# Layer 1 of a two-layer attention kernel: the key mask moves from TensorE to VectorE, the conditioning's scale and shift from VectorE and GpSimd to ScalarE

## The reference, cut to what matters

```python
xn = _ln(x, ln_w, ln_b)
q = xn @ Wq + bq
k = xn @ Wk + bk + (1.0 - src_mask) * -1000000.0
q = softmax(q.reshape(b, t, h, dh), axis=-1)
k = softmax(k.reshape(b, t, h, dh), axis=1)
v = ((xn @ Wv + bv) * src_mask).reshape(b, t, h, dh)
att = einsum('bnhd,bnhl->bhdl', k, v)
y = einsum('bnhd,bhdl->bnhl', q, att).reshape(b, t, d)
scale, shift = split((silu(emb) @ W_emb + b_emb)[:, None, :], 2, axis=2)
hh = _ln(y, ln2_w, ln2_b) * (1.0 + scale) + shift
return x + silu(hh) @ W_out + b_out
```

## Time and profile before

| what | value |
|---|---|
| median of 3 runs | 1095.91 us (1095.82 to 1096.64) |
| the profiled execution, its own time | 1097.78 us |
| its span, first to last instruction | 1096.0 us |
| TensorE busy | 1054.8 us, 96% of the span |
| VectorE, ScalarE, GpSimd busy | 759.8, 591.6, 448.6 us |
| mean granted TensorE clock | 0.993 of full speed |

### The profile page before, as it was taken

How to read it: one execution, slowest core, us unless ns; L and a number is a source line. 1 busy time by engine, 2 the same in 40 slices (tenths; PEclk the granted TensorE clock), 3 DMA queues, 4 the chain that set the end, 5 groups by cost and what they waited for, 6 DMA issues and landing times. The chain is left out here.

```text
span 1096.0 us, 25953 instructions
## 1 busy us (share of the span) xinstructions
PE 1054.8 (96%) x8696; PEld 909.8 (83%) x8696; DVE 759.8 (69%) x1326; ACT 591.6 (54%) x1960; POOL 448.6 (41%) x783
## 2 busy tenths in 40 slices
PE   6999999999999999999999999999999999999995
PEld 4878888888888888888887778888888888888884
DVE  4656766676666766667678787777777777777764
ACT  5366667776677766776588443433343443434431
POOL 3242434334343343433343344444444444444432
PEclk9999999999999999999999999999999999999997
DMA  8824110111101111011102211111111111111011
GB/s 275 256 84 141 42 61 24 62 62 41 60 24 62 62 41 59 25 62 63 43 23 98 95 50 33 40 55 57 57 57 57 57 57 57 52 52 39 31 38 58
DMA packets 46017, 71.65 MB, mean 65 GB/s; under 512 B 10256, under 2 KB 14448, under 8 KB 45968
## 3 DMA queue, kind: packets, MB, share of 16 engines
q1 hardware_dynamic: 45968, 71.02, 20.3%
HBM read 54.19 MB, written 16.79 MB: 65 GB/s over the span
## 5 line engine op out<-in xcount | busy, mean ns | idle before, releaser
L1276 PE MATMUL bank<-xt_hi,w_hi 128*128 128x256 f32 x768 | 228.4, 297 | 3.1 <-DVE xt_lo L893 3.1
L1277 PE MATMUL bank<-xt_lo,w_hi 128*128 128x256 f32 x768 | 218.5, 284 | 0.0
L1278 PE MATMUL bank<-xt_hi,w_lo 128*128 128x256 f32 x768 | 218.3, 284 | 0.0
L454 POOL TENSOR_SCALAR stat<-stat 128x1 f32<-128x1 f32 x128 | 34.5, 270 | 441.8 <-DVE stat L884 417.7
L613 ACT ACTIVATE prob<-prob,neg_max 128x128 f32<-128x128 f32 x512 | 198.7, 396 | 6.7 <-DVE neg_max L907 6.6
L632 ACT ACTIVATE th<-z_s 128x512 f32<-128x512 f32 x64 | 40.5, 633 | 249.9 <-POOL z_s L488 249.8
L1276 PE MATMUL bank<-w_hi,xt_hi 128*128 128x512 f32 x384 | 158.3, 412 | 1.0 <-DVE w_lo L835 1.0
L1276 PEld LDWEIGHTS bank<-xt_hi,w_hi 128*128 128x128 f32 x768 | 148.9, 194 | 9.1 <-DVE w_lo L835 4.8
L1278 PE MATMUL bank<-w_hi,xt_lo 128*128 128x512 f32 x384 | 150.5, 392 | 0.0
L1277 PE MATMUL bank<-w_lo,xt_hi 128*128 128x512 f32 x384 | 149.8, 390 | 0.0
L1277 PEld LDWEIGHTS bank<-xt_lo,w_hi 128*128 128x128 f32 x768 | 148.6, 193 | 0.0
(11 more groups left out here) (130 smaller groups left out, 2203.3 us busy)
## 6 DMA issues: line engine op xcount, KB each, us to landing
x_in<-in_x_dram SPq DMA_DIRECT2D x32, 256.0 KB, 2.8
x_res<-in_x_dram SPq DMA_DIRECT2D x32, 256.0 KB, 2.9
between_layers<-x_res SPq DMA_DIRECT2D x32, 256.0 KB, 2.0
x_in<-between_layers SPq DMA_DIRECT2D x32, 256.0 KB, 2.8
x_res<-between_layers SPq DMA_DIRECT2D x32, 256.0 KB, 2.8
out_dram<-x_res SPq DMA_DIRECT2D x32, 256.0 KB, 2.6
room<-in_L_cond_W_emb_dram SPq DMA_DIRECT2D x8, 512.0 KB, 7.3
prob<-in_L_cond_emb_w_dram SPq DMA_DIRECT2D x4, 512.0 KB, 7.5
```

The source lines that it names most:

```text
L454: pool.tensor_scalar(v[:, 8:9], v[:, 7:8], EPS, None, ALU.add).then_inc(s[a_in].sem, 1)
L1276: pe.matmul(o, a_hi, b_hi, start=start, stop=False)
L1277: pe.matmul(o, a_hi, b_lo, start=False, stop=False)
L1278: return pe.matmul(o, a_lo, b_hi, start=False, stop=stop)
```

## The change

On TensorE the four mask matmuls of a pair go, and with them `mask_wide`, `ones_parts`, `mask_parts` and what fills them. The mask bias of layer 1 is now saved to DRAM as layer 0's is, and `load_mask_pair` (SP) fetches it for each pair, spread over all partitions, into the one tile `mask_pair` (128 x 256). In `k_soft` VectorE takes each key block out of the bank itself, adding the key bias and the mask in one instruction (`scalar_tensor_tensor`), before it takes the maximum; ScalarE's `k_out` stays in layer 0 alone. In layer 1 `film_scale` and `add_shift` go; ScalarE's new `film1` does scale and shift in four instructions of 128 columns out of the bank, ahead of the tanh. In the mixed step `k_soft(f, 0)` stands earlier in VectorE's list.

```diff
@@ SP
+            def load_mask_pair(f):
+                sp.wait_ge(*done(s["kb_out"], f + (-GROUP)))
+                at = f + (-B)
+                flat = mask_bias[1].rearrange("(o b) p -> o (b p)", o=1)
...
+                sp.dma_start(mask_pair[:], row.broadcast_to([P, N])).then_inc(s["mask_pair_in"].sem, 16)
...
                 if k:
                     load_back(1, k, 1)
+                if n:
+                    load_mask_pair(n)
+                if k:
                     store(1, k, 0)
@@ GpSimd
                 if k:
                     norm2(k, 1)
-                    add_shift(1, k, 0)
-                    add_shift(1, k, 1)
@@ ScalarE
+            def film1(k, b):
+
+                at = k + (b - B)
+                act.wait_ge(*done(s["h_pe"], k + b))
+                act.wait_ge(*done(s["s_full"], k + (b - 2)))
+                for c in range(C):
...
+                    last = act.activation(z_s[:, b, c * P:(c + 1) * P], bank[SECOND["H"][b]][:, c * P:(c + 1) * P],
+                                          ACT.Identity, bias=shift, scale=scale)
+                last.then_inc(s["z_full"].sem, 1)
...
                 if f:
-                    k_out(1, f, slot, 0)
                     k_exps(f, slot, 0)
...
                 if f:
-                    k_out(1, f, slot, 1)
                     k_exps(f, slot, 1)
...
                 if k:
+                    film1(k, 0)
                     tanh(k, 0)
                 if f:
                     q_exps(f, slot, 0)
                 if k:
                     s_high(k, 0)
+                    film1(k, 1)
                     tanh(k, 1)
@@ VectorE
             def k_soft(f, slot, pair):
-                dve.wait_ge(*done(s["ka_out" if pair == 0 else "kb_out"], f))
+                if pair == 0:
+                    dve.wait_ge(s["mask_pair_in"].sem, (f + (-B)).value() * (16 // GROUP) + 16)
+                out = s["ka_out" if pair == 0 else "kb_out"]
+                dve.wait_ge(*done(s["ka_pe" if pair == 0 else "kb_pe"], f))
...
+                for j in range(2):
+                    c = 2 * pair + j
+                    last = dve.scalar_tensor_tensor(out=kv[:, c, :], in0=from_bank[:, j, :], scalar=col[:, 1, KB, c:c + 1],
+                                                    in1=mask_pair[:], op0=ALU.add, op1=ALU.add)
+                last.then_inc(out.sem, GROUP)
+                dve.wait_ge(*done(out, f))
...
@@ VectorE, step_mixed
                 softmax(k, 0, (3,))
+                dve.wait_ge(bias_dve, TURN[1, WK])
+                k_soft(f, slot, 0)
                 stats1(n, 0)
                 softmax(k, 1, (0, 1, 2))
                 output(FIRST, late + (-1), 1)
                 softmax(k, 1, (3,))
-                k_soft(f, slot, 0)
                 k_soft(f, slot, 1)
@@ VectorE, step1
                     y_norm(1, k, 1 - slot, 1)
-                    film_scale(1, k, 0)
...
                     s_low_part(k, 0)
-                    film_scale(1, k, 1)
@@ TensorE, project
-                    if l == 1:
...
-                        pe.matmul(o, ones_parts[:], cols, start=True, stop=False)
```

More of the change, by code:

```diff
@@ L79, in build @@
     WQ, WK, WV, WO = range(4)
-    mask_bias = nc.dram_tensor("mask_bias", [B, P], F32, kind="Internal").ap()
+    mask_bias = [nc.dram_tensor(f"mask_bias{l}", [B, P], F32, kind="Internal").ap() for l in range(2)]
     middle = nc.dram_tensor("between_layers", [B, T, D], F32, kind="Internal").ap()
@@ L365, in start @@
                 load_wide(1, WO, OUT_BIAS[1])
[L366 to L370, removed]
+                sp.wait_ge(mask_cut, 4)
+                sp.dma_start(mask_bias[1], mask_tmp[1][:, P:2 * P]).then_inc(mask_saved, 16)
                 sp.wait_ge(bias_sum_pe, 3)
@@ L441, in _ @@
             pool.memset(ones_32nd[:], 1.0 / 32).then_inc(once, 1)
[L442 to L447, removed]
+            pool.wait_ge(once, 4)
             pool.tensor_tensor(pick[:], ident[:, 0:2 * B], ident[:, 2 * B:4 * B], ALU.add).then_inc(consts, 1)
@@ L626, in y_t_out @@
                 act.activation(y_t[:], bank[FIRST["PV"][b]][:], ACT.Copy).then_inc(s["pv_out"].sem, 1)
+            def film1(k, b):
[3 more added lines that the diff above has]
+                for c in range(C):
+                    scale, shift = (film_ab[:, 1, i, c, at.const:at.const + 1] if at.reg is None
+                                    else film_ab[:, 1, i, c, bass.ds(at.value(), 1)] for i in range(2))
+                    last = act.activation(z_s[:, b, c * P:(c + 1) * P], bank[SECOND["H"][b]][:, c * P:(c + 1) * P],
+                                          ACT.Identity, bias=shift, scale=scale)
+                last.then_inc(s["z_full"].sem, 1)
             def tanh(k, b):
@@ L712, in step0 @@
                 exps(k, 1, (3,))
[L713 removed]
+                k_out(f, slot, 1)
                 if i == G - 2:
@@ L720, in step0 @@
                 y_t_out(k, 1)
+                if i == 0:
+                    act.wait_ge(mask_saved, 32)
                 tanh(k, 0)
@@ L1047, in step0 @@
                 if late:
-                    film_scale(0, late + (-1), 1)
+                    film_scale(late + (-1), 1)
                 if i == G - 3:
```

84 lines of the change are left out of this document (35 added, 49 removed).

## The result

The changed kernel takes 1105.26 us (median of 6 runs, 1104.44 to 1106.32) against 1096.73 us before: a ratio of 1.0076, 95% interval 1.0063 to 1.0089. It is slower by 0.8%, and the forecast was 1092.0 us.

What follows compares the result with a forecast made beforehand. TensorE was taken to bound layer 1 (busy 434.68 of 440 us), the chain's latency the end. Terms 0 - 0.2 - 0.55 - 3.1 = -3.9 us from 1095.9 gave 1092.0 us; range 1086.5 to 1100.0.

Steps and rivals of the forecast that it cites:

- rival 5: The mask's fetch comes late and `k_soft` waits for it in each step, by 1 us: 1105 us; chance 0.03.
- Masks on TensorE: In each layer 1 step, dropping TensorE's mask matmuls saves 0.40 us (0.16 to 0.48).
- The wait for the low part: At sequence 1's output, `film1` brings VectorE's low part earlier and TensorE's wait goes: -0.31 us a step.
- The late chain: VectorE's evictions add 0.88 us before the second `turn_yn`, where 0.45 were free: TensorE waits 0.43 us a step.
- The meetings: At the second `turn_yn`, silu against GpSimd: whoever starts first, half the steps each; wait 0.43 or 1.0, taken as 0.72 us.
- rival 3: Difference and silu both hold up GpSimd; TensorE waits some 1.4 us at the second `turn_yn`: 1101.1 us; chance 0.15.
- A step: Steps 17 to 29: -0.40 - 0.31 + 0.72 = 0.0 us each, nothing over the 13.
- The mixed step: `k_soft` puts 1.76 us ahead of `y_norm(k, 0)`, which had 1.34 us idle: +0.6 us (0 to 1.2).
- From there to step 17: Step G: masks -0.24, waits at `turn_yn` and outputs -1.07, later `norm2(k, 1)` +0.5; -0.8 us in all.
- Step 30 and the end: Step 30 gains 0.55 us, as `norm2` is not late; in the last step outputs come earlier: -3.1 us.
- The mask's fetch and the start: Fetch of `mask_pair` at no cost, issued early; at the start TensorE waits for weights and inputs: nothing (0 to -0.5).

Runs made afterwards that it cites:

- film_only: The kernel before with `film1` (scale and shift on ScalarE), TensorE's masks and ScalarE's `k_out` as they were: 1089.56 us, ratio 0.9926.
- idle_reduce: The changed kernel plus one VectorE reduction, its result unread, ahead of the first sequence's query maximum: 1093.33 us, ratio 0.9962.
- sum_in_bank: The changed kernel with query plus bias left in the bank, so maximum and difference read PSUM instead of SBUF: 1095.75 us, ratio 0.9984.
- mixed_early: The changed kernel with the mixed step's `k_soft(f, 1)` moved up behind the second of sequence 1's four softmax parts: 1104.27 us, ratio 1.0053.
- tail_wait: The changed kernel with GpSimd's last residual waiting, in the last step, for VectorE's low part of the sequence before: 1102.98 us, ratio 1.0051.

## Why the prediction was wrong

It named the right place, the right wait and the right mechanism, and gave 0.19 to a slower kernel; its central number was off by 13 us, on the other side. The measured 1105.26 us is near rival 5's 1105, but that is luck: no `k_soft` of layer 1 waits for its mask. Term by term, in spans (+7.8 us in all, 1.6 of it ahead of the mixed step, where the forecast had nothing):

- *Masks on TensorE*, forecast -0.40 us a step: -0.35. `film_only`, which keeps them, has 0.23 us more in the first pair of blocks and 0.12 in the second.
- *The wait for the low part*, forecast -0.31: -0.40, all gone as said. `film1` takes 1.50 us, nearer to four instructions in a row (1.56) than to the 1.3 I took.
- *The late chain*, forecast +0.43 at the second `turn_yn`: +0.33 or +0.40 where it stands by itself in `idle_reduce`, +0.45 or +0.53 in `sum_in_bank` (3.66 or 3.74 us between the two `turn_yn`, in turn).
- *The meetings*, forecast +0.29 more (0.72 in all): **+0.75** by GpSimd's rows (1.26 in all). This is the step that failed: "Who is first is decided by less than 0.1 us ... I take half of the steps each way". It treated the outcome as a coin for each step. The engines keep nearly the same distance from step to step (the difference starts 0.01 to 0.03 us ahead of the power in 11 of the 13 steps), so the same one wins in these each time. And it priced a single meeting, where the difference meets the power (+0.52) and the silu then meets the normalisation (+0.23). That is rival 3, which I held at 0.15 on the ground that two or three such instructions are fewer than four. Its wait of 1.4 us is near the 1.26 lost (1.10 by TensorE's row); its total of 1101.1 was too low by what the other places cost. Its sign, a step above 30.4 us, is the one that came.
- *A step*, forecast 0.0: +0.54 by the rows, +6.5 over the 13, two of which have only a part of the meetings.
- *The mixed step*, forecast +0.6 (0 to 1.2): +2.1, the second step that failed. The prediction set 1.76 us of evictions against 1.34 of idle time. It left out VectorE's wait for `x_in`, which the fetch of `mask_pair` precedes (0.83 us, and 1.21 in `mixed_early`), and did not ask who needs the bank that the keys lie in. `mixed_early` is without the bank's wait and still +1.86, so VectorE's way is the larger part. *From there to step 17*, forecast -0.8: -0.85, though step G's second `turn_yn` waits 1.58 us.
- *Step 30 and the end*, forecast -3.65: -1.6. The changed kernel lost 0.46 and 1.04 us to two more meetings, which the prediction had not looked for there. `tail_wait`, without the second, has -3.1 for the last stretch, but at the higher clock, so that it bears out the chain only in part.
- *The mask's fetch and the start*, forecast nothing: no `k_soft` waits for the fetch, but in the mixed step `x_in` lands later behind it (7.4 us after its issue instead of 5.7). At the start the rows show nothing that the other kernels confirm, the clock aside.

The range ended at 1100.0, since it took in only half of rival 3 and no rival let the misses of the separate places add up. Those of the loop and of the last step had one cause, the port; the mixed step's had others.

## What to carry to other kernels

In these traces a VectorE instruction with both inputs in SBUF stopped a GpSimd instruction that started just behind it, even one on a single column (0.57 us became 1.09). Before work is moved between engines, list those instructions against GpSimd's chain, at their new times, and ask which pairs meet; a meeting repeats from step to step (11 of 13 here). Then the cheap cures are to read one input from PSUM, or to reorder so that GpSimd's chain starts earlier. And when an engine takes over an eviction, look who writes that bank next; when a transfer is added, look which one lands later behind it.

## What the runs showed of the hardware that I had not expected

- An instruction more on VectorE, which set the next one 0.21 us later, made a step 0.8 us shorter (29.69 against 30.49). More work on an engine that is not the bound can be faster.
- GpSimd's instruction on 128x1 is stopped for as long as one on 128x512: 0.52 us on the power and 0.50 on the normalisation, beside the same difference of 0.69 us.
- Two meeting instructions can both go at full length: with the power 0.07 to 0.17 us (`idle_reduce`) or 0.24 us (at 734 us) ahead of the difference, 0.57 and 0.69 us. Of those that started so close, only the power did; GpSimd's long ones made VectorE wait (1.30 us, 1.02 us in `idle_reduce`).
- The granted clock differed in the same stretch of the same layer-0 code (0.66 and 0.83 between 86 and 96 us), and 1.4 us went there with it.
